# A perceiver block: the last context tiles of two batches share one keys tile, and tiles become 12 of 128 tokens and one of 65

## The reference

```
q = rmsnorm((layernorm(x) @ Wq).reshape(8, 64, 16, 128), gq)
k = rmsnorm((ctx @ Wk).reshape(8, 1601, 16, 128), gk)
v = (ctx @ Wv).reshape(8, 1601, 16, 128)
attn = softmax(einsum("bqhd,bkhd->bhqk", q, k) / sqrt(128))
x = x + einsum("bhqk,bkhd->bqhd", attn, v).reshape(8, 64, 2048) @ Wo
x = x + causal_self_attention(layernorm(x))     # 16 heads of 32
x = x + ternary_swiglu_ffn(layernorm(x))        # weights rounded to three values by groups of 64
```

## Time and profile before

| | us |
|---|---|
| median of 3 runs | 1484.35 |
| the profiled execution | 1483.59 |
| its span, first to last instruction | 1481.4 |
| PE busy | 1462.9 (99%) |
| DVE busy | 1244.1 (84%) |
| ACT busy | 1010.8 (68%) |
| POOL busy | 167.1 (11%) |

### The profile page before, as it was taken

One profiled execution on the slowest core, in us unless ns is written; L12 is line 12 of the kernel. 1 busy time (PEld: TensorE's weight loads), 2 busy tenths in 40 slices (PEclk: granted clock), 3 DMA queues, 4 the chain that ended last, 5 costly groups with the idle time before them and its releaser, 6 DMA issues.

```text
span 1481.4 us, 22365 instructions
## 1 busy us (share of the span) xinstructions
PE 1462.9 (99%) x6901; PEld 1196.3 (81%) x6901; DVE 1244.1 (84%) x2003; ACT 1010.8 (68%) x3767; POOL 167.1 (11%) x117
## 2 busy tenths in 40 slices
PE   9999999999999999999999999999999999999998
PEld 7778878888888888888888888888888877788887
DVE  8746888989999999899899989988898899677543
ACT  5676777776777777777767776777677666656432
POOL 2210000002000200010010002000200210123342
PEclk9999999999999999999999999999999999999999
DMA  6542332222222122213222222211111132841000
GB/s 199 174 136 78 114 97 70 91 71 69 81 86 79 60 86 86 79 59 93 83 71 68 88 76 61 79 54 46 57 57 46 43 115 89 281 173 59 1 0 29
DMA packets 103751, 125.25 MB, mean 85 GB/s; under 512 B 11593, under 2 KB 78161, under 8 KB 102481
## 3 DMA queue, kind: packets, MB, share of 16 engines
q1 hardware_dynamic: 96336, 116.49, 25.2%
q10 hardware_dynamic: 7296, 7.34, 1.5%
HBM read 101.16 MB, written 22.64 MB: 84 GB/s over the span
## 4 chain that ended last, share of the span: by engine, by line
PE 84%; DVE 9%; issue 2%; ACT 2%; DMA 1%; SPq 0%; POOL 0%; ACTq 0%; DVEq 0%; POOLq 0%
PE ps L36 26%; PE ps L37 26%; PE ps L38 26%; PE ps L953 2%; PE ps L954 2%; DVE p_lo L42 1%; DVE ring L1191 1%; PE ps L971 1%; PE ps L972 1%; DVE ring L1162 1%; DMA row_raw<-in_wp 1%; PE ps L826 1%; DVE wq_lo L42 0%; DMA wq_raw<-in_wq 0%; PE ps L594 0%
## 5 line engine op out<-in xcount | busy, mean ns | idle before, releaser
L1777 ACT ACTIVATE ps<-ps 123x128 f32<-123x128 f32 (+1 forms) x1248 | 326.2, 261 | 150.5 <-PE ps L38 147.1
L36 PE MATMUL ps<-wk_hi,cT_hi 128*128 128x512 f32 x832 | 327.0, 393 | 2.8 <-ACT ps L1777 2.5
L37 PE MATMUL ps<-wk_lo,cT_hi 128*128 128x512 f32 x832 | 325.9, 392 | 0.0
L38 PE MATMUL ps<-wk_hi,cT_lo 128*128 128x512 f32 x832 | 323.8, 389 | 0.0
L1777 ACT ACTIVATION_READ_ACCUMULATOR ps<-ps 123x1 f32 (+1 forms) x1248 | 231.1, 185 | 0.0
L36 PEld LDWEIGHTS ps<-wk_hi,cT_hi 128*128 128x128 f32 x832 | 156.2, 188 | 41.3 <-ACT ps L1777 3.4
L38 PEld LDWEIGHTS ps<-wk_hi,cT_lo 128*128 128x128 f32 x832 | 156.3, 188 | 34.0
L37 PEld LDWEIGHTS ps<-wk_lo,cT_hi 128*128 128x128 f32 x832 | 156.6, 188 | 32.2
L36 PE MATMUL ps<-fq_hi,cT_hi 128*128 128x512 f32 x416 | 162.0, 389 | 0.1
L38 PE MATMUL ps<-fq_hi,cT_lo 128*128 128x512 f32 x416 | 161.9, 389 | 0.0
L37 PE MATMUL ps<-fq_lo,cT_hi 128*128 128x512 f32 x416 | 161.9, 389 | 0.0
(11 more groups left out here) (241 smaller groups left out, 2663.8 us busy)
## 6 DMA issues: line engine op xcount, KB each, us to landing
cT_raw<-in_ctxT SPq DMA_DIRECT2D x96, 128.0 KB, 3.4
cn_raw<-in_ctx SPq DMA_DIRECT2D x88, 123.0 KB
row_raw<-in_wgu SPq DMA_DIRECT2D x32, 256.0 KB, 2.8
w_raw<-in_wguT SPq DMA_DIRECT2D x32, 256.0 KB, 2.7
qk_scratch<-folded ACTq DMA_DIRECT2D x8, 896.0 KB, 4.2
fq_raw<-qk_scratch SPq DMA_DIRECT2D x14, 512.0 KB, 3.8
pc_scratch<-pc_out SPq DMA_DIRECT2D x7, 1024.0 KB, 5.7
w_scale<-scale_scratch SPq DMA_DIRECT2D x96, 64.0 KB, 2.7
```

Of the source, the lines that this page charges most:

```text
L36: pe.matmul(dst, l_hi, r_hi, start=first, stop=False)
L37: pe.matmul(dst, l_hi, r_lo, start=False, stop=False)
L38: return pe.matmul(dst, l_lo, r_hi, start=False, stop=last)
L1777: done = act.activation(head, head, ACT.Square, accum_out=k_sum[0:n, i, g * GH + h:g * GH + h + 1])
```

## The change

A batch is now 12 tiles of 128 tokens and a last one of 65. The last tile of every batch holds 64 tokens of its own in one half of the partitions (the lower half for even batches, the upper for odd) and in the other half the 1601st tokens of all batches of the same parity, four of them, with zeros behind. Batches 0 and 1 compute the keys of such a tile as they are. For batches 2 and 3 (4 and 5, 6 and 7) one tile that holds 64 tokens of each gets its keys at the even batch, and the inverse roots are kept in `left_rstd` for both; the roots of the 1601st tokens are there from batches 0 and 1. Steps 51, 77 and 103 (the last tile of batches 3, 5 and 7) then have no keys: no `key_bank`, `key_square`, `key_guess`, `key_mean`, and no `key_refine` in the step behind. The scores of a last tile are scaled with one operation that also adds -1e30 to the rows that are not the batch's (`left_mask`, made once by POOL).

The even batches 2, 4 and 6 load two transposed tiles for their last tile: one for the keys and one for the scores. So there are three more loads, high parts and low parts, two of each in steps 37, 63 and 89. Pieces of batches 3 and 5 stand at t = 10 instead of t = 12. POOL's fill of the running maximum and sum goes, since all tiles have 128 rows.

```diff
-        rows = [TK // TT + (t < TK % TT) for t in range(TT)]
-        tiles = [(b, t, rows[t]) for b in range(B) for t in range(TT)]
+        REST = TT - 1
+        tiles = [(b, t, P) for b in range(B) for t in range(TT)]
+        halves = (slice(0, P // 2), slice(P // 2, P))
+        key_tiles = [s for s, (b, t, n) in enumerate(tiles) if t < REST or b < 2 or b % 2 == 0]
+        key_of = {s: i for i, s in enumerate(key_tiles)}
+        cT_seq, cT_keys, cT_scores, cT_step = [], {}, {}, []
+        for s, (b, t, n) in enumerate(tiles):
+            if t == REST and b >= 2 and s in key_of:
+                cT_keys[s] = len(cT_seq)
+                cT_seq.append((s, True))
+                cT_step.append(s - 2)
+                cT_scores[s] = len(cT_seq)
+                cT_step.append(s - 1)
+            else:
+                cT_keys[s] = cT_scores[s] = len(cT_seq)
+                cT_step.append(s - 2)
+            cT_seq.append((s, False))
...
-            b * TT + t for b in range(1, B - 1) for t in (3, 5, 6, 8, 9, 11, 12)][:NP - TT + ROW_LEAD]
+            b * TT + t for b in range(1, B - 1)
+            for t in ((3, 5, 6, 8, 9, 11, 12) if b * TT + REST in key_of else (3, 5, 6, 8, 9, 10, 11))][:NP - TT + ROW_LEAD]
...
                 if half == 0:
+                    pe.wait_ge(cT_lo_done, cT_scores[s] + 1)
...
-                    if s > 0 or g > 1:
+                    if s in key_of and (s > 0 or g > 1):
                         key_bank(s, g)
...
+                elif b < 2:
+                    dve.scalar_tensor_tensor(out=left_rstd[:, b], in0=w[:], scalar=1.5, in1=y,
+                                             op0=ALU.add, op1=ALU.mult).then_inc(k_refined, 1)
+                else:
+                    dve.wait_ge(scaled, (b - 1) * TT + REST + 1)
+                    for parity, rows in enumerate(halves):
+                        dve.scalar_tensor_tensor(out=left_rstd[rows, parity], in0=w[rows], scalar=1.5, in1=y[rows],
+                                                 op0=ALU.add, op1=ALU.mult).then_inc(k_refined, 1)
...
+                if t < REST:
+                    rstd = k_rstd[:, key_of[s] % 2].unsqueeze(2).broadcast_to([P, H, TQ])
+                    dve.tensor_tensor(dst, raw, rstd, ALU.mult).then_inc(scaled, 1)
+                else:
+                    rstd = left_rstd[:, b % 2].unsqueeze(2).broadcast_to([P, H, TQ])
+                    dve.scalar_tensor_tensor(out=dst, in0=raw, scalar=left_mask[:, b % 2, b // 2:b // 2 + 1], in1=rstd,
+                                             op0=ALU.add, op1=ALU.mult).then_inc(scaled, 1)
...
-                if s > 0:
+                if s - 1 in key_of:
                     key_refine(s - 1)
...
-                if s + 2 < N and tiles[s][1] > 0:
-                    low_cT(s + 2)
+                for e in [e for e in range(len(cT_seq)) if cT_step[e] == s and tiles[s][1] > 0]:
+                    low_cT(e)
...
-                key_mean(s)
+                if s in key_of:
+                    key_mean(s)
...
-            key_refine(N - 1)
             scale_scores(N - 1)
...
-            pool.memset(run_max[P // 2:], -3.0e38).then_inc(consts, 1)
-            pool.memset(run_sum[P // 2:], 0.0).then_inc(consts, 1)
+            for parity, rows in enumerate(halves):
+                single = halves[1 - parity]
+                pool.memset(left_mask[rows, parity], 0.0).then_inc(consts, 1)
+                pool.tensor_scalar(left_mask[single, parity], ident[single, single.start:single.start + B // 2], LEFT_OUT,
+                                   -LEFT_OUT, ALU.mult, ALU.add).then_inc(consts, 1)
```

More of the change, by code:

```diff
@@ L415, in perceiver_block, with refinements @@
         sum_count = max_count
+        def refinements(s):
+            return sum(4 if tiles[k][1] == REST and tiles[k][0] >= 2 else 3 for k in key_tiles if k <= s)
         def evacuations(b, part=None):
@@ L1132, in key_mean @@
             def key_mean(s):
[L1133 to L1139 removed]
+                k = key_of[s]
@@ L1142, in key_refine @@
             def key_refine(s):
-                i, n = s % 2, tiles[s][2]
-                y, w = k_rstd[0:n, i], k_step[0:n]
-                dve.wait_ge(k_guessed, 2 * (s + 1))
-                dve.tensor_tensor(w, y, y, ALU.mult).then_inc(k_refined, 1)
-                dve.wait_ge(k_refined, 3 * s + 1)
-                dve.scalar_tensor_tensor(out=w, in0=w, scalar=-0.5, in1=k_mean[0:n, i],
-                                         op0=ALU.mult, op1=ALU.mult).then_inc(k_refined, 1)
-                dve.wait_ge(k_refined, 3 * s + 2)
@@ L1152, in key_refine @@
-                dve.scalar_tensor_tensor(out=y, in0=w, scalar=1.5, in1=y,
-                                         op0=ALU.add, op1=ALU.mult).then_inc(k_refined, 1)
+                b, t, n = tiles[s]
+                i = key_of[s] % 2
+                y, w = k_rstd[:, i], k_step
+                done = refinements(s - 1)
+                dve.wait_ge(k_guessed, 2 * (key_of[s] + 1))
+                dve.tensor_tensor(w[:], y, y, ALU.mult).then_inc(k_refined, 1)
+                dve.wait_ge(k_refined, done + 1)
@@ L1372, in dve_program @@
                     ternary_round(piece_at[s])
-                if s + 2 < N and tiles[s][1] == 0:
-                    low_cT(s + 2)
+                for e in [e for e in range(len(cT_seq)) if cT_step[e] == s and tiles[s][1] == 0]:
+                    low_cT(e)
                 for u in slots:
@@ new lines, in key_guess @@
+                k = key_of[s]
+                act.wait_ge(k_var, k + 1)
+                act.activation(k_log[:], k_mean[:, k % 2], ACT.Ln).then_inc(k_guessed, 1)
+                act.wait_ge(k_guessed, 2 * k + 1)
+                if k >= 2:
+                    before = key_tiles[k - 2]
+                    if tiles[before][1] < REST:
+                        act.wait_ge(scaled, before + 1)
+                    else:
+                        act.wait_ge(k_refined, refinements(before))
+                act.activation(k_rstd[:, k % 2], k_log[:], ACT.Exp, scale=-0.5).then_inc(k_guessed, 1)
@@ L2467 @@
     arr = {k: np.asarray(v) for k, v in inputs.items()}
+    ctx, half = arr["ctx_1024"], 64
+    pairs = range(2, ctx.shape[0], 2)
+    rest = np.zeros((ctx.shape[0], 2 * half, ctx.shape[2]), ctx.dtype)
+    for b in range(ctx.shape[0]):
+        own, single = (0, half) if b % 2 == 0 else (half, 0)
+        rest[b, own:own + half] = ctx[b, -half - 1:-1]
+        rest[b, single:single + ctx.shape[0] // 2] = ctx[b % 2::2, -1]
+    both = np.stack([np.concatenate([ctx[b, -half - 1:-1], ctx[b + 1, -half - 1:-1]]) for b in pairs])
     laid_out = {
@@ L2471 @@
         "ctxT": arr["ctx_1024"].transpose(0, 2, 1),
+        "rest": rest,
+        "restT": np.concatenate([rest, both]).transpose(0, 2, 1),
         "wq": arr["L0_xattn_Wq"],
```

146 lines of the change are left out of this document (76 added, 70 removed).

## The result

The changed kernel takes 1467.26 us (median of 4 runs, 1466.27 to 1469.55) beside 1484.36 for the kernel before: ratio 0.9887, interval 0.9873 to 0.9901. The forecast was 1479.0 with a range down to 1475.5, so the direction was right and the size was not: 17.1 us went where I had summed 5.3, and even the lower end lies 8 us above the result.

The account below looks back on a forecast made before the run. The prediction took PE to bound the loop, with DVE right behind. Its terms, -7.0 - 1.5 + 1.2 + 0.3 + 1.7 = -5.3 us, took 1484.35 to 1479.0 us, with an 8-in-10 range of 1475.5 to 1482.0.

Parts of the forecast that it names:

- The step that failed: All tiles: 128 rows in place of 123 cost nothing on DVE or PE, so priced at no change.
- Odd edges: Steps 51 and 77: PE loses 5.49 us of keys, waits 1.97 for `p_lo`; 3.5 us gained each, -7.0 in all.
- DVE's lag: Steps 49 and 50: unbroken pieces put DVE 0.48 us later, so `p_lo` comes late and PE waits 1.97 us.
- The clock: PE's two new waits in steps 51 and 77: one fall to half clock likeliest, +1.7 us.
- the rule cited in the prediction: PE's clock falls only for idle gaps well longer than these waits; no-fall rival 1477.3 us, chance 0.28.
- Even edges: Batches 2, 4 and 6: a second low part and split root store delay DVE, which has no slack; +1.2 us.
- Masked scaling: Last tiles' scores, eight times: one operation with a column as scalar costs 0.04 us more each, +0.3 us.
- the slower rival: Masked scaling takes a second pass over 1024 columns, 1.22 us more eight times; 1488.5 us, chance 0.06.
- Step 103: End of the loop: DVE bounds, and `k_sum`, `k_mean` and the root leave its path; -1.5 us.
- The sum: Whole kernel: -7.0 - 1.5 + 1.2 + 0.3 + 1.7 = -5.3 us, giving a median of 1479.0 us.

Follow-up runs that it names:

- b128: Kernel before with all 13 tiles of a batch at 128 rows, neighbours overlapping; nothing shared, no mask, no step without keys: 1474.86 us, ratio 0.9934.
- rows123: Changed kernel with the weighted context's matmuls contracting over rows 0 to 122 alone, all else at 128 rows: 1473.45 us.
- cols123: Changed kernel with the loop's weighted context computed for 123 of each 128 context features, 128 rows contracted; step 37 read, no total time given.
- ctx12: rows123 with all twelve weighted-context matmuls in one piece behind the third keys bank, in place of six and six: 1486.18 us.
- before_in: Kernel before with the changed kernel's two further inputs declared in the same place but not used: 1482.28 us in one execution.
- all_keys: Changed kernel with new tiles and masked scaling, but every last tile computes its own keys; pieces at t = 12 in all batches: 1472.46 us, ratio 0.9917.
- fill1: Changed kernel with PE making the next tile's first keys bank between scores and weighted context in steps 51 and 77: 1464.07 us.
- shift: Changed kernel with transposed context tiles 0 to 11 loaded from five tokens later: 1468.86 us.
- odd12: Changed kernel with the pieces of batches 3 and 5 back at t = 12 in place of t = 10: 1468.59 us.
- one_cT: Changed kernel with last tiles of batches 2, 4 and 6 computing keys from the transposed tile the scores use, without a second load: 1470.16 us.
- fill2e: Changed kernel with two keys banks made ahead in steps 51 and 77, pieces of batches 3 and 5 at t = 2, 3, 5, 6, 8, 9, 10: 1465.94 us.
- fill2: Changed kernel with PE making two keys banks of the next tile ahead in steps 51 and 77: 1462.78 us, ratio 0.9858.

## Why the prediction was wrong, step by step

**The step that failed** is the sentence that 128 rows in place of 123 cost nothing, "PE streams 512 columns either way". It left out the price of a change of shape. Each of some 90 steps had four or six of them: by the starts of the scores, b128 gains 8.5 us between tiles 14 and 101, and 9.9 in its runs (about 1 us of that is not found in the steps of the two profiles). rows123 and cols123 bring the dearer steps back in a kernel whose tiles have 128 rows, and ctx12 shows that the number of changes sets the price. The miss was 1479.0 - 1467.3 = 11.7. The sign of it stood in the earlier trace rows: 0.229 on average over the step, 0.225 for the scores.

**A second term was not seen**: 1.3 us at the first edge, reproduced by before_in with tensors that are not even read. The trace of the kernel before shows the wait (1.55 us) but not that the list of inputs sets it. A further 0.9 us of the profiles' difference of 15.7 is there before the loop's first scores (99.88 us after, 100.76 before); that start varies from 99.88 to 101.51 among the variants and is no gain.

**Odd edges.** Forecast 3.5 each. Batch 3, all_keys against the changed kernel: 1.36 + 1.58 = 2.94. Keys are 24 x 0.2267 = 5.44 and not 5.49; between starts PE loses 604.94 to 607.54, 2.60 less the 0.23 of one matmul, 2.37 where I had 1.97. The mechanism was right, DVE's lag 0.4 larger. That 0.4 hangs on the failed step too: in rows123, whose steps last 10.99 us as before, PE loses 2.15 - 0.23 = 1.92, and the two steps of the edge are 1.39 + 2.07 = 3.46 shorter than its others, at both edges the 3.5 of the forecast. With steps of 10.88 PE comes to the wait earlier, and DVE, which takes 11.05 us a step with a piece, does not follow. With 1.36 us of work in the wait (fill1) 1.25 more comes at each, which confirms it from the other side. Batch 5 gives 1.36 and no more, by the clock.

**The clock.** Forecast: one fall in the loop at 1.7 us. It came, and costs 1.6: shift has the fall at the first wait and not at the second, and its starts lie 1.62 us later in the one place and 1.60 earlier in the other. Length alone does not decide. At the odd edges of the profiled variants, behind one wait of 2.94 us between starts no fall followed, behind two of 2.72 (ctx12) one, behind seven of 2.59 or 2.60 five, behind six of 2.15 to 2.17 two, behind four of 1.82 or less (fill1, odd12) none. The new wait of PE in step 103 (below) stands with 2.42 to 2.49 us in eleven profiles, and the clock fell behind six of them. In the changed kernel's profile it did, a second fall that the forecast did not have:

```profile
1189.07:1192.47 3.40, 3.40 (x10) 2.71 (x11) 3.40 (x4) 1.54 (x3) 0.00 (x0) 0.63 0.02 5
```

The forecast counted the fall at the end of the loop as there before. That one, behind 1221.51 in the kernel before, has no counterpart in the changed kernel's profile. So the rule cited in the prediction (the Trainium skill, "TensorE: Matmul & The Clock Gate", section "HAM oscillation — how this bites in real kernels") does not hold here: these waits are shorter than the gaps it names, and the clock falls behind six of the ten of 2.59 us or more.

**Even edges.** Forecast +1.2, measured 0.16. A low part of 0.34 us on an engine I called without slack reached PE at one edge of three, with 0.2 (one_cT). The DVE rows without gaps there do not prove that something waits for their end.

**Masked scaling.** Forecast +0.3. 1.28 us against 1.22 eight times is 0.5 on DVE, and all_keys against b128 shows 0.15 on the path between tiles 14 and 101. The second pass of the slower rival is out.

**Step 103.** Forecast -1.5. From the maximum of tile 102 to the scaling of tile 103 DVE takes 4.73 us, 5.57 in all_keys: the five rows are gone, 1.4 us, but the scaling now waits 0.56 for scores that PE makes at half clock, behind its own wait:

```profile
1189.07 0.47 PE L36 MATMUL ps<-fq_hi,cT_hi 128*128 128x512 f32 x1 [2.10 <-DVE ring L1209]
```

```profile
1193.68 1.28 DVE L1214 SCALAR_TENSOR_TENSOR ring<-ps,left_mask,left_rstd 128x1024 f32<-128x1024 f32 x1 [0.56 <-PE ps L38]
```

0.84 is what is left there. The half clock is not part of the mechanism, for where it does not follow, the forecast comes out. DVE in fill2e, from the same maximum on:

```profile
1187.00 1.22 DVE L1235 TENSOR_TENSOR run_max<-run_max,ring 128x1024 f32<-128x1024 f32 x1
...
1191.08 1.28 DVE L1217 SCALAR_TENSOR_TENSOR ring<-ps,left_mask,left_rstd 128x1024 f32<-128x1024 f32 x1
```

4.08 us, as in fill2 and odd12, 1.5 less than 5.57, and the last scaling waits for nothing. The first product behind the weighted context (`pc_hi` by `wv_hi`) then stands 57.6 us behind the scores of tile 101, with the fall 58.3 and in all_keys 59.1. At the end of the program none of it is seen, since the stretch from that product to the end lasts 233.7 us in all_keys and 234.5 in the changed kernel. It lies between 233.7 and 235.0 in the five profiles whose step 103 has keys and between 234.3 and 235.3 in the twelve without; whether the gain is lost there or only covered, no run shows. A wait of PE for the ring in place of PE's own work was not in my list for this step.

**The sum.** What I had summed for sharing was -7.0 - 1.5 + 1.2 + 1.7 = -5.6, the mask left out. Between the profiles of all_keys and of the changed kernel, from tile 14 to the end, it is -4.1, between the medians -5.2. In the profiles the parts are -5.9 (odd edges, the fall taken out), 0.0 (end), +0.2 (even edges) and +1.6 (the fall): errors of +1.1, +1.5, -1.0 and -0.1. They cancel in part, and that the medians give -5.2 beside -5.6 is in part luck. The other 11.9 us of the result's 17.1 belong to two things that I priced at nothing: the tiles' shape, 9.9 from the kernel before to b128, and the two more inputs with what else sets the first edge, 2.4 from b128 to all_keys; that makes 12.3, and 0.4 is the difference of the kernel before between the sets of runs. Of the 2.4, 2.05 arise at the first edge, where b128 stands 0.65 us behind the kernel before; before_in brings the kernel before to the length that all kernels with the two inputs have there.

## What to carry to other kernels

When an average over a step (0.229) differs from the price of one group in it (0.225), find the group that is dearer before using either; here 2% of a matmul was worth 9.9 us, about twice what I had summed for the whole change. On PE, keep all matmuls of a loop at one full shape, and where that can't be, put those of one shape side by side if no engine is held up by it (ctx12 halved the changes and was 12.7 us slower than rows123, for its waits). A wait that a removed stretch of work uncovers is worth filling with work of the next step, up to the point where the next engine in the chain is late.
